# A mixer layer on one core: three more turns on VectorE, a third dense bank, the low part of the gated y on GpSimd

## What is computed

```python
proj = xn @ in_proj_w.T                       # gate, x, B, C, dt
xBC = silu(conv4(proj[x, B, C]))
dt = softplus(dt + dt_bias); dA = exp(dt * A)
state = state * dA + (dt * x) outer B         # per token, state 64 x 128 per head
y = state @ C + x * D
yn = y * rsqrt(mean(y * y, group) + EPS) * norm_weight
out = (yn * silu(gate)) @ out_proj_w.T        # gated y, then projected
h = einsum(xn, A); lora = einsum(h, w_top2, B) * 2
result = x + out + (xn @ W_base.T + b_base + lora)
```

## Time and profile before

| | us |
|---|---|
| median of three runs | 3176.2 (3176.06 to 3176.92) |
| the profiled execution, as timed | 3177.18 |
| its span in the profile | 3175.3 |
| TensorE busy | 3157.5 (99%) |
| VectorE busy | 2469.2 (78%) |
| ScalarE busy | 1550.1 (49%) |
| GpSimd busy | 857.4 (27%) |
| TensorE's clock granted | 1.00 of full speed |

### The profile page before, as it was taken

How to read it: one execution, slowest core, us unless ns; L and a number is a source line. 1 busy time by engine, 2 the same in 40 slices (tenths; PEclk the granted TensorE clock), 3 DMA queues, 4 the chain that set the end, 5 groups by cost and what they waited for, 6 DMA issues and landing times.

```text
span 3175.3 us, 55177 instructions
## 1 busy us (share of the span) xinstructions
PE 3157.5 (99%) x17933; PEld 2598.2 (82%) x17933; DVE 2469.2 (78%) x4773; ACT 1550.1 (49%) x3816; POOL 857.4 (27%) x917
## 2 busy tenths in 40 slices
PE   8999999999999999999999999999999999999999
PEld 7788888887888888888788888888878888888887
DVE  7977777786588888888658888888855888888883
ACT  5666656663364444454235544445423545444441
POOL 4444434343032222222102222222210222222220
PEclk9999999999999999999999999999999999999999
DMA  8777777776665555556476555556557655555554
GB/s 288 273 269 263 265 276 261 277 258 255 238 208 183 189 187 192 187 187 209 160 234 201 185 188 189 196 181 194 196 170 237 193 192 186 192 189 197 183 189 159
DMA packets 185666, 672.63 MB, mean 212 GB/s; under 512 B 21056, under 2 KB 22208, under 8 KB 185408
## 3 DMA queue, kind: packets, MB, share of 16 engines
q1 hardware_dynamic: 161280, 584.91, 54.6%
q10 hardware_dynamic: 24128, 84.42, 7.9%
HBM read 532.41 MB, written 136.84 MB: 211 GB/s over the span
## 4 chain that ended last, share of the span: by engine, by line
PE 95%; DVE 3%; ACT 1%; DMA 1%; issue 0%; SPq 0%; ACTq 0%; DVEq 0%
PE dense L1040 27%; PE dense L1042 27%; PE dense L1041 27%; PE pY L1140 3%; PE pD L1170 2%; PE pD L1140 1%; DVE conv_us L1452 1%; PE pCB L1116 1%; PE pU L1040 1%; PE dense L1077 1%; PE pS L1041 1%; PE pS L1040 1%; PE pU L1042 1%; PE pS L1042 1%; PE pU L1041 1%; PE pX L1110 1%
## 5 line engine op out<-in xcount | busy, mean ns | idle before, releaser
L1040 PE MATMUL dense<-xn_hi,w_hl 128*128 128x512 f32 (+1 forms) x2888 | 1143.2, 396 | 1.4 <-POOL w_hl L437 0.8
L1042 PE MATMUL dense<-xn_hi,w_hl 128*128 128x512 f32 (+1 forms) x2888 | 1125.1, 390 | 0.0
L1041 PE MATMUL dense<-xn_lo,w_hl 128*128 128x512 f32 (+1 forms) x2888 | 1123.6, 389 | 0.0
L1042 PEld LDWEIGHTS dense<-xn_hi,w_hl 128*128 128x128 f32 (+1 forms) x2888 | 540.1, 187 | 115.7
L1040 PEld LDWEIGHTS dense<-xn_hi,w_hl 128*128 128x128 f32 (+1 forms) x2888 | 540.7, 187 | 114.4 <-issue 3.0
L1041 PEld LDWEIGHTS dense<-xn_lo,w_hl 128*128 128x128 f32 (+1 forms) x2888 | 540.9, 187 | 110.9 <-issue 1.9
L1452 DVE SCALAR_TENSOR_TENSOR conv_us<-conv_in,const_g,conv_us 128x512 f32<-128x512 f32 x576 | 466.2, 810 | 138.8 <-ACT conv_us L686 123.2
L1040 PE MATMUL dense<-z_hi,w_hl 128*128 128x512 f32 x1024 | 406.0, 397 | 1.9 <-DVE acc L1606 1.4
L1042 PE MATMUL dense<-z_hi,w_hl 128*128 128x512 f32 x1024 | 399.3, 390 | 0.0
L1041 PE MATMUL dense<-z_lo,w_hl 128*128 128x512 f32 x1024 | 398.7, 389 | 0.0
L493 POOL TENSOR_TENSOR C_lo<-BC,C_hi 128x128 fp32r<-128x128 f32 x120 | 73.5, 613 | 1191.0 <-ACT S_hi L724 1190.3
(11 more groups left out here) (205 smaller groups left out, 4610.1 us busy)
## 6 DMA issues: line engine op xcount, KB each, us to landing
w_hl<-w_split SPq DMA_DIRECT2D x732, 512.0 KB, 3.5
w_split<-w_hl SPq DMA_DIRECT2D x244, 512.0 KB, 3.6
cum_b<-cum_scratch ACTq DMA_DIRECT2D x128, 512.0 KB, 5.0
w_raw<-w_slots_dram SPq DMA_DIRECT2D x122, 512.0 KB, 5.2
acc<-x_tr_dram ACTq DMA_DIRECT2D x16, 512.0 KB, 6.0
out_tr_dram<-acc ACTq DMA_DIRECT2D x16, 512.0 KB, 4.7
BC<-x_tok_dram SPq DMA_DIRECT2D x6, 512.0 KB, 5.0
conv_us<-x_tok_dram SPq DMA_DIRECT2D x6, 512.0 KB, 5.8
```

Source lines behind the costliest of these rows:

```text
L1040: nc.tensor.matmul(out, lhs[0], rhs[0], start=start, stop=False)
L1041: nc.tensor.matmul(out, lhs[0], rhs[1], start=False, stop=False)
L1042: return nc.tensor.matmul(out, lhs[1], rhs[0], start=False, stop=stop)
```

## The change

All of it concerns the 21 paired groups, but for the banks of the tail.

1. **Turns.** `BY_DVE` becomes (0, 1, 2, 3) and `B_tm` holds four chunks: TensorE's four turns of x (chunk 1) and its one turn of B (chunk 0) go. VectorE turns x of chunk 1 in pieces between the gates and the first output halves, where the turns of B stood; B of all four chunks of a group is turned at the end of the group before, half ahead of `gated(g, 2)`, half ahead of `prep`.
2. **Banks.** `pX`, free now, becomes a third bank for dense units; a unit waits for the unit three before it. The transposes of the layer norm use `pS` in its place.
3. **Low part.** `z_lo` is made by GpSimd (`z_low`), four times in each paired group; `gated_lo` goes from VectorE's paired groups.

```diff
-        B_tm = sb("B_tm", [128, NC - 1, N])
+        B_tm = sb("B_tm", [128, NC, N])
...
-        ln_banks = [pCB, pX, pU, pY]
-        ln_banks_first = ln_banks + [pD0, pS]
+        ln_banks = [pCB, pS, pU, pY]
+        ln_banks_first = [pCB, pX, pU, pY, pD0, pS]
+        def turn_bank(unit):
+            return (pX, bank[1], bank[0])[unit % 3]
...
-        BY_DVE = (0, 2, 3)
+        BY_DVE = (0, 1, 2, 3)
...
+                def z_low(g, c):
+                    pool.wait_ge(zhi_done, chunk(q, g, c) + 1)
+                    cs = slice(c * Q, (c + 1) * Q)
+                    nc.gpsimd.tensor_tensor(z_lo[:, :, cs], z_t[:], z_hi[:, :, cs].bitcast(F32), ALU.subtract)\
+                        .then_inc(z_done, 1)
...
                 def paired_group(g, p, last=False):
                     chunk_pre(g, p, 0)
                     wx_low(g, 0)
+                    z_low(g - 1, 3)
                     chunk_pre(g, p, 1)
                     wx_low(g, 1)
                     inv_rms(g, 0, True)
                     inv_rms(g, 1, True)
                     chunk_pre(g, p, 2)
                     wx_low(g, 2)
+                    z_low(g, 0)
                     chunk_pre(g, p, 3)
+                    z_low(g, 1)
                     wx_low(g, 3)
...
                     inv_rms(g, 3, True)
+                    z_low(g, 2)
...
-                    if two and c > 0:
+                    if two:
                         act.wait_ge(bt_done, bt_n(q, g))
...
+                    elif two:
+                        pe.wait_ge(evac_act, act_n(q, g - 1, 7 + j) if j < 3 else act_n(q, g, j - 3))
...
+                        ahead = 3 if two else 2
...
-                    chunk_1(g, 0, p, 0 in BY_DVE, False)
-                    gate_unit(g, False, 2)
+                    chunk_1(g, 0, p, True, True)
+                    gate_unit(g, False, 2, True)
...
-                    chunk_1(g, 1, p, 1 in BY_DVE, True)
-                    out_units(g, 1)
+                    chunk_1(g, 1, p, True, True)
+                    out_units(g, 1, two=True)
...
                     gate_tile(g, 1, False)
-                    gated_lo(g - 1, 3)
                     gate_tile(g, 2, False)
...
+                    x_rows(g, 1, p, 0, 1)
                     y_state(g, 0, True)
...
-                    B_rows(g, p, 0, 1)
-                    out_adds(g, 0, halves=(0,))
-                    B_rows(g, p, 1, 3)
-                    out_adds(g, 0, halves=(1,))
-                    B_rows(g, p, 3, 4)
+                    x_rows(g, 1, p, 1, 2)
+                    out_adds(g, 0, halves=(0,), two=True)
+                    x_rows(g, 1, p, 2, 4)
+                    out_adds(g, 0, halves=(1,), two=True)
...
+                    if not last:
+                        B_rows(g + 1, 1 - p, 0, 2)
                     gated(g, 2)
                     save_state(g)
-                    gated_lo(g, 2)
...
                         silu(g, 5, 1 - p)
+                        B_rows(g + 1, 1 - p, 2, 4)
                         prep(g + 1)
```

More of the change, by code:

```diff
@@ L588, in paired_group @@
                     inv_rms(g, 3, True)
-                    if last and not last_block:
-                        ln_inv(q + 1, 2)
-                        ln_inv(q + 1, 3)
+                    z_low(g, 2)
+                    if last:
+                        if not last_block:
+                            ln_inv(q + 1, 2)
+                        z_low(7, 3)
+                        if not last_block:
+                            ln_inv(q + 1, 3)
                 group(0, 0, first=True)
@@ L1076, in more, with out_units @@
                             pe.wait_ge(evac_dve, ffn_n(q, 0))
-                            return nc.tensor.matmul(bank[(K_X + j) % 2][:], lora_sb[:, (j - 1) * 128:j * 128], w_tok[:],
+                            return nc.tensor.matmul(b[:], lora_sb[:, (j - 1) * 128:j * 128], w_tok[:],
                                                     start=False, stop=True)
-                    in_unit(7, K_X + j, (K_X + j) % 2, more)
-                def out_units(g, m, tail=False):
+                    in_unit(7, K_X + j, b, more)
+                def out_units(g, m, tail=False, two=False):
                     k = (K_TAIL if tail else K_OUT) + m
@@ L1095, in out_units @@
                         weights(g, k, h)
-                        b = ((K_TAIL if tail else 3) + i) % 2
+                        b = turn_bank((0 if tail else 4) + i) if two else bank[((K_TAIL if tail else 3) + i) % 2]
                         for t in range(KZ):
-                            mm = three(bank[b][:], w(k, 4 * h + t), (z_hi[:, t, :], z_lo[:, t, :]), t == 0, t == KZ - 1)
+                            mm = three(b[:], w(k, 4 * h + t), (z_hi[:, t, :], z_lo[:, t, :]), t == 0, t == KZ - 1)
                         mm.then_inc(dense_done, 1)
@@ L1903, in group @@
                             silu(g, 5, 1 - p)
+                        if not first_block:
+                            B_rows(g + 1, 1 - p, 0, 4)
                         prep(g + 1)
@@ L1908, in x_unit @@
                         if last:
[L1909 removed]
+                            ffn_evac(j, True)
                         else:
@@ L2017, in block_body @@
                 for m in range(4):
-                    out_adds(7, m, tail=True)
+                    out_adds(7, m, tail=True, two=not first_block)
                     if m < 2:
```

128 lines of the change are left out of this document (67 added, 61 removed).

## The result

| | before | after |
|---|---|---|
| median, us | 3176.56 (3176.06 to 3177.28, 4 runs) | 3211.13 (3210.36 to 3212.22, 4 runs) |
| ratio | | 1.011, 95% interval 1.0097 to 1.0123 |
| span of the profile | 3175.3 | 3208.6 |

A forecast was written before the change was run, and what follows sets the result against it. TensorE was taken as the bound, so only its own work and new waits count. Profiled 3177.18 - 11.5 (turns) + 9.0 (place 1) + 7.3 (place 2) = 3182.0; from the 1.0 lower median, forecast 3181.0 us, range 3165.5 to 3191.5.

The forecast's parts named there:

- The turns: TensorE loses its B turn (0.11 us) and four x turns (0.44 us) in each of 21 groups: 11.5 us gone.
- place 1: TensorE's state update of chunk 3: z_lo ahead of wx_lo on GpSimd makes it 0.75 us later in 12 groups, 9.0 lost.
- The third bank: Dense units: no gain by itself, as TensorE waits for no bank; lets VectorE empty a bank one unit later.
- Place 2: TensorE's first output unit, needing z_lo of the previous group's last chunk: 0.35 us later in 21 groups, 7.3 us lost.
- VectorE first: At place 2, VectorE's second gate tile goes ahead of GpSimd's z_lo, which then ends at 1042.7 against TensorE's 1042.43.
- I keep 3.3: At the group border, VectorE's time from z_t of chunk 2 to the x turns stays 3.3 us, before eight added transposes.
- the chain moves with TensorE: At place 1, GpSimd's chain cannot start sooner: its z_t and taps waited 1.69 us for ScalarE's copy of TensorE's unit.
- The yn of chunk 1: Possible unpriced TensorE wait for the turned yn of chunk 1, whose bank VectorE frees later than before.
- (a): Rival: no new wait at either place, only TensorE's saved work counts; 3164.7 us, chance 14%.
- (c): Rival: S_lo and decay on GpSimd still slow VectorE's dtx and wx, adding 0.5 us per group; 3191.5 us, 20%.
- (b): Rival: GpSimd's z_lo gets in between VectorE's gate tiles, so place 2 costs nothing; 3173.7 us, 23%.
- (d): Rival: GpSimd's low part holds up VectorE everywhere and the turns bring nothing; within a few us of 3176, 3%.

The follow-up runs named there:

- e12: e10 with the last four transposes of chunk 3's x turn moved behind z_t of chunk 1: 3166.05 us, ratio 0.9967 to the kernel before.
- e8: Changed kernel with the third dense bank taken back, turns and GpSimd's low part as changed: 3244.41 us.
- e3: Changed kernel with all low parts of the gated y back on VectorE at their old places, turns and third bank as changed: 3185.22 us, ratio 1.0031.
- e2: Changed kernel with VectorE's second eight B transposes moved ahead of the last silu: 3187.75 us, ratio 1.0038.
- e4: Kernel before with only the low parts moved to GpSimd, in the changed kernel's order, turns and banks as before: 3183.36 us, ratio 1.0023.
- e1: Changed kernel with GpSimd's wx_lo of chunk 3 put ahead of z_lo of chunk 1 again: 3209.95 us.
- e5: Changed kernel with the edits of both e1 and e2: 3186.62 us.
- e6: e5 with half of chunk 3's x turn (8 of 16 transposes) moved behind z_t of chunk 1: 3184.13 us.
- e10: Changed kernel with e1's order, last silu before B's last quarter, half chunk 3's x turn before second taps, four chunk 1 x transposes between gate tiles: 3169.83 us.

## Why the prediction was wrong, step by step

**The turns: right.** The matmuls fell by 105, from 17933 to 17828. In `e12`, where 0.8 us of waits at place 1 are left, the kernel is 9.8 us faster than before, with an interval of 6.7 to 14.3 by its ratio; 11.5 less 0.8 lies in it. In its last block, where neither place has a wait left, a group takes 88.32 us from one first output unit to the next, 88.85 before: 0.53 of the foretold 0.55.

**The third bank: half right.** "Gives nothing by itself" was not tried alone. What was said of its use, that VectorE may be later, was right, and `e8` prices it at 33.3 us.

**Place 2: the size was wrong, 1.18 to 1.36 instead of 0.35 (23.4 us instead of 7.3).** How far ahead of TensorE's earliest start each step lies; that start is foretold at 1042.43, and in the changed kernel it is 1936.27 less 1.18, 1935.09:

| step | foretold, us ahead | measured, us ahead |
|---|---|---|
| z_t of chunk 2 starts | 17.33 | 17.23 |
| x turns start | 11.53 | 10.64 |
| z_t of chunk 3 starts | 3.03 | 2.15 |
| z_lo of chunk 3 ends | -0.27 | -1.07 |

All of the 0.8 arises between the first step and the second; the others keep their distance. "VectorE first" at the gate tiles came true (z_lo took 1.80), and so did the return from dtx and wx. But the evidence for "VectorE first" was one-sided. GpSimd's decay in the earlier trace rows was asked for at 1033.64, 0.39 before wx started, as C_lo was 0.39 before z_lo; it ended at 1035.01, and wx behind it took 1.53. There GpSimd went first. No run here shows what decides between the two, so this step was partly luck. The step that failed is "z_lo leaves, but the last silu behind it must wait for ScalarE as long, so I keep 3.3". The silu waits as foretold, but GpSimd's new `z_lo` of chunk 2 is asked for while it does, and the silu takes 1.36 instead of 0.68. I had costed this operation at two of its four places only. In `e3`, without the collision, z_t to the x turns takes 5.99 with a low part of VectorE in it, against 6.59; in `e2`, where neither the silu's standing nor the collision is left, the wait at place 2 is gone. No run takes away the collision and nothing else, so its 0.68 is read from the rows.

**Place 1: 1.18 instead of 0.75, and the cause was misjudged.** From C_lo's start to the end of wx_lo the forecast had 5.88 us, and the row shows 5.66 (1891.06 to 1896.72), so the order on GpSimd alone was right but for 0.22: 0.75 foretold, and 0.52 in `e4`, where turns and banks are those of before. What failed is "so the chain moves with TensorE". In the earlier trace rows VectorE had 1.69 us to spare ahead of the taps, and I took this for a cover that stays. With the turn of chunk 1 the border's lateness is carried to the middle of the group: VectorE's z_t of chunk 0 is late, ScalarE's z_hi waits for it, and the evacuation of the second x unit stands behind. Against the last matmul into `pS`, C_lo starts 4.36 us ahead (1895.42 - 1891.06); before it was 5.02 (that matmul came 0.23 before the one at 1093.79 of the earlier trace rows, and C_lo at 1088.54): 0.66 late. 0.75 - 0.22 + 0.66 is 1.19, the wait that the row shows, and `e1` and `e3` have 0.64 for the lateness by itself. With the turn of chunk 3 in pieces and the other orders of `e12` it falls to 0.07, with the same work on VectorE.

**The yn of chunk 1** was named as a place where I could be wrong, without a price: 2.6 us, and the linear layer's w_tok another 2.0. They are 1.3 and 0.1 in `e2`, where only the border changed, and both are gone in `e6`, once the turn of chunk 3 is split too: they were VectorE's lateness again.

**The sum was built wrongly too.** I added waits of places as if each were a cost of its own. `e1` and `e5` show that they are not: the order of VectorE and ScalarE across one group closes on itself, from place 2 over the taps to the next place 2. While VectorE was the late one, a wait taken from one place came back at the next (0.54 less at place 1, 0.45 more at place 2). The parts cost 9.4 and 7.5 us apart (`e3`, `e4`) and 35 together.

**Rivals.** (a) had 14% and its time is what the best order gives; what spoke against it, the order of one queue, was a matter of order only. (c) named the right kind of cause, a collision of VectorE and GpSimd that moves, but at the wrong place: S_lo and the decay did not meet dtx and wx at the border (the decay ended 1.3 us ahead of dtx). Its 3191.5 was still 20 us too low. (b) did not happen, as the 1.80 shows, and (d) is out by its time.

What stays open: the 1.36 of place 2 in the last block, where place 1 is absent, was not taken apart by itself.

## What to carry over

When an edit makes one engine later at one point, follow its lateness once round the whole loop, to the same point of the next round, and ask at each idle stretch on the way whether it is still as long; a sum of local waits held here only while nobody but the bound engine was late. Each operation given to another engine has to be costed at every place where it runs, with what its neighbour does at that moment: here work of two kinds, one that meets GpSimd (silu, taps, gate tiles) and one that doesn't (transposes), could be exchanged for nothing. And a long block of work without waits, such as 16 transposes, belongs in the idle stretches in pieces; the same instructions took from 3211 to 3166 us by their order alone.

## What was unexpected of the hardware

The transposes of 32 x 128 on VectorE keep their pace beside GpSimd's subtractions: eight took 2.53 us with `z_lo` running beside half of them (`e2`) and 2.52 without it (the changed kernel, 1921.17), while a silu beside the same `z_lo` took 1.36 instead of 0.68. Nor do they hold GpSimd up: `z_lo` took 1.29 beside them (`e10`) and 1.80 beside the gate tiles. The Trainium skill, page "SBUF — State Buffer", section "Who interferes with whom", says that a VectorE instruction with at most one SBUF input, outside its 2-port modes, does not contend with GpSimd. These rows agree, and this difference is what `e2` and `e10` made use of.
